# A four-layer attention and feed-forward kernel: the stack of a batch filled in four portions, its repeated rows stored once, four places for rows of maxima

## What is computed

```python
x = x + jnp.tanh(g_xattn[l]) * xattn_l(_layernorm(x, axis=-1), ctx_1024, ctx_1024)

# xattn, with 16 heads of 16 features, batch 8, 256 queries and 256 keys
scores = jnp.einsum('bhqd,bhkd->bhqk', q, k) / jnp.sqrt(16)
attn = jax.nn.softmax(scores, axis=-1)
x = jnp.einsum('bhqk,bhkd->bhqd', attn, v)
```

## Time and profile before

| | |
|---|---|
| Median of 3 runs | 1998.75 us (1997.51 to 2001.54) |
| The profiled execution's own time | 1983.74 us |
| Its span | 1981.9 us |
| Mean granted TensorE clock | 0.868 |
| TensorE matmul busy | 1470.5 us (74%) |
| VectorE busy | 1083.2 us (55%) |
| ScalarE busy | 735.4 us (37%) |
| GpSimd busy | 544.0 us (27%) |
| Moved by DMA | 202.65 MB, mean 102 GB/s |

### The profile page before, as it was taken

The page is one execution under the profiler, slowest core; times in us unless marked ns, Lnnn a source line. Parts: engine busy times, 40 slices in busy tenths (PEclk is TensorE's granted clock), DMA queues, the critical chain, the costliest instruction groups (busy, mean ns, idle before and its releaser), DMA issues.

```text
span 1981.9 us, 29494 instructions
## 1 busy us (share of the span) xinstructions
PE 1470.5 (74%) x9789; PEld 1035.4 (52%) x9816; DVE 1083.2 (55%) x2363; ACT 735.4 (37%) x1458; POOL 544.0 (27%) x519
## 2 busy tenths in 40 slices
PE   1489959986777349997996477942899755788676
PEld 1245548853445248887884244521788523455334
DVE  5256563346565515554537466581455556565797
ACT  2145644324555113332321255620344213554342
POOL 4342220021220353345315222007443431222000
PEclk9989979996789679998998688975999986779897
DMA  9989420099980241322126999012432593980000
GB/s 307 239 221 83 34 67 1 1 303 151 79 66 20 77 155 58 133 77 69 37 73 225 224 72 91 2 53 98 158 103 85 160 275 95 87 66 2 0 11 32
DMA packets 153868, 202.65 MB, mean 102 GB/s; under 512 B 19968, under 2 KB 113542, under 8 KB 153736
## 3 DMA queue, kind: packets, MB, share of 16 engines
q0 software_dynamic: 75392, 95.15, 33.7%
q1 hardware_dynamic: 78368, 106.05, 16.7%
HBM read 120.25 MB, written 80.35 MB: 101 GB/s over the span
## 4 chain that ended last, share of the span: by engine, by line
PE 48%; DMA 17%; DVE 15%; issue 8%; POOL 4%; ACT 4%; another core or an unknown queue 2%; SPq 2%; DVEq 0%; ACTq 0%; POOLq 0%
DMA stack<-mt 11%; PE PS L852 5%; PE PS L792 4%; PE PS L892 3%; PE PS L827 3%; PE PS L1030 2%; PE PS L1032 2%; PE PS L1031 2%; PE PS L1008 2%; PE PS L1009 2%; PE PS L1007 2%; PE PS L1018 2%; DVE xng L1583 2%; DVE amx L2139 1%
## 5 line engine op out<-in xcount | busy, mean ns | idle before, releaser
L1709 DVE TENSOR_REDUCE nm<-PS 128x2 f32<-128x512 f32 x512 | 336.8, 683 | 261.3 <-PE PS L792 165.5
L792 PE MATMUL PS<-stack 48*128 48x256 f32 x1024 | 154.9, 387 | 107.0 <-DVE nm L1709 56.4
L545 POOL DMA_DIRECT2D stack<-mt x128 | 70.0, 547 | 506.4 <-ACT mt L1294 505.8
L792 PEld LDWEIGHTS PS<-stack 48*128 48x128 f32 x1024 | 94.9, 228 | 204.8 <-DVE nm L1709 108.9
L1285 ACT ACTIVATE probs<-PS 128x512 f32<-128x512 f32 x256 | 139.0, 595 | 64.7 <-PE PS L835 31.8
L1285 ACT ACTIVATE xng<-PS 128x512 f32<-128x512 f32 x256 | 138.3, 591 | 46.6 <-PE PS L835 23.9
L852 PE MATMUL PS<-probs,vpad 128*32 128x256 f32 x1024 | 85.8, 462 | 71.3 <-ACT mt L1294 69.2
L827 PE MATMUL PS<-stack 49*128 49x256 f32 x1024 | 121.9, 319 | 19.7 <-DMA stack<-mt 15.2
L1031 PE MATMUL PS<-whi,hl 128*128 x468 | 133.2, 285 | 0.0
L1032 PE MATMUL PS<-wlo,hh 128*128 x468 | 133.2, 285 | 0.0
L1030 PE MATMUL PS<-whi,hh 128*128 x468 | 133.1, 284 | 0.0
(11 more groups left out here) (289 smaller groups left out, 3394.8 us busy)
## 6 DMA issues: line engine op xcount, KB each, us to landing
stack<-qk_parts POOLq DMA_DIRECT2D x128, 384.0 KB, 10.4
qk_parts<-k_parts SPq DMA_DIRECT2D x48, 512.0 KB
qk_parts<-q_parts SPq DMA_DIRECT2D x48, 512.0 KB, 10.9
wslot<-W_dram POOLq DMA_DIRECT2D x16, 1024.0 KB, 8.9
ys_sorted<-yo SPq DMA_DIRECT2D x78, 128.0 KB, 1.7
wide<-ctxT_dram SPq DMA_DIRECT2D x16, 512.0 KB, 5.8
wslot<-W_dram POOLq DMA_DIRECT2D x16, 512.0 KB, 6.1
xg<-xs_sorted SPq DMA_DIRECT2D x62, 128.0 KB, 2.1
```

The source lines that it names most:

```text
L792: mm = pe.matmul(PS[:, (2 * t + h) % 3, qt * S:(qt + 1) * S], q[rows, qt * P:(qt + 1) * P], kk[rows], start=(l > 0 or qt == 0), stop=(l > ...
L1709: nc.vector.tensor_reduce(nm[:, j % 2, at:at + 2], PS[:, (2 * t + h) % 3, :].rearrange("p (q n) -> p q n", q=2), AX.X, ALU.max, negate=Tru ...
```

## The change

Three things. The high parts are stored once: two stores for a group's keys and two for its queries in place of three each. The stack of a batch is filled in four portions (keys h 0, keys h 1, queries h 0, queries h 1) of two transfers each (16 rows, then 32 rows), one portion behind each row of maxima. And `mt` has four places with a semaphore each.

```diff
-        mt = sb("mt", [8, 2, P], F32R, at)
+        mt = sb("mt", [8, 4, P], F32R, at)
...
-                for r, part in enumerate((k_hi(g), k_hi(g), k_lo(g))):
+                for r, part in enumerate((k_hi(g), k_lo(g))):
...
-                for r, part in enumerate((q_hi(g), q_lo(g), q_hi(g))):
+                for r, part in enumerate((q_hi(g), q_lo(g))):
...
-            def load_stack(l, b):
-
-                if b >= SLOTS:
+            def load_stack(l, b, at):
+
+                of, h = (1, 0)[at // 2], at % 2
+                if at == 0 and b >= SLOTS:
                     pool.wait_ge(sc_mm, 2 * STEPS * l + 2 * PAIRS * (b - SLOTS + 1))
-                else:
+                if at == 0 and b < SLOTS:
                     nc.gpsimd.dma_start(stack[MAXROW:MAXROW + 65:64, b % SLOTS, 1].rearrange("p c n -> p (c n)"),
                                         io["ones_rows"]).then_inc(stack_in[b % SLOTS], 16)
-                for n, out in ((1, k_out), (0, q_out)):
-                    pool.wait_ge(*stored(out, l, b // 2))
-                    for h in range(2):
-                        nc.gpsimd.dma_start(stack[64 * h:64 * h + MAXROW, b % SLOTS, n],
-                                            parts[n, h][:, :, b * S:(b + 1) * S]).then_inc(stack_in[b % SLOTS], 16)
+                pool.wait_ge(*stored((q_out, k_out)[of], l, b // 2))
+                rows = lambda r, n: stack[64 * h + DH * r:64 * h + DH * (r + n), b % SLOTS, of]
+                part = parts[of, h][:, :, b * S:(b + 1) * S]
+                first, both = (0, 1) if of else (2, 0)
+                nc.gpsimd.dma_start(rows(first, 1), part[0:DH]).then_inc(stack_in[b % SLOTS], 16)
+                nc.gpsimd.dma_start(rows(both, 2), part).then_inc(stack_in[b % SLOTS], 16)
...
-                load_stack(l, 1)
-                load_stack(l, 2)
+                load_stack(l, 1, 0)
                 for n in range(QUADS):
...
                     put_rows(l, n)
-                    if n % 4 == 3 and n >= 7 and n // 4 + 2 < B:
-                        load_stack(l, n // 4 + 2)
+                    if (n + 5) // 4 < B:
+                        load_stack(l, (n + 5) // 4, (n + 1) % 4)
...
-                    pe.wait_ge(stack_in[b % SLOTS], 64 * loads + 16 * (l + 1))
+                    pe.wait_ge(stack_in[b % SLOTS], 128 * loads + 16 * (l + 1))
...
-                if j >= 2:
-                    act.wait_ge(row_in[j % 2], 16 * (j // 2))
-                nc.scalar.activation(mt[:, j % 2, :], PS[0:8, 6, S:S + P], ACT.Identity).then_inc(mt_done, 1)
+                if j >= 4:
+                    act.wait_ge(row_in[j % 4], 16 * (j // 4))
+                nc.scalar.activation(mt[:, j % 4, :], PS[0:8, 6, S:S + P], ACT.Identity).then_inc(mt_done, 1)
```

More of the change, by code:

```diff
@@ L259, in build @@
         ys = nc.dram_tensor("ys_sorted", (NT * P, D), F32, kind="Internal").ap()
-        parts = nc.dram_tensor("qk_parts", (2, 2, MAXROW, PAIRS, T), F32, kind="Internal").ap()
+        parts = nc.dram_tensor("qk_parts", (2, 2, 2 * DH, PAIRS, T), F32, kind="Internal").ap()
         PS = ctx.enter_context(nc.psum_tensor("PS", [P, 8, 512], F32))
@@ L279, in build @@
         stack_in = sem("stack_in", SLOTS)
-        mt_done, row_in = sem("mt_done"), sem("row_in", 2)
+        mt_done, row_in = sem("mt_done"), sem("row_in", 4)
         nat_mm, max_done = sem("nat_mm"), sem("max_done")
@@ L332, in stored @@
             n = GROUPS * l + g
-            return out[n % 2], 48 * (n // 2 + 1)
+            return out[n % 2], 32 * (n // 2 + 1)
         def rows_of(n, r, g):
@@ L545, in put_rows @@
                 nc.gpsimd.dma_start(stack[MAXROW:MAXROW + 65:64, b % SLOTS, 0, c:c + 2, :].rearrange("p c n -> p (c n)"),
-                                    mt[:, j % 2, :]).then_inc(row_in[j % 2], 16)
+                                    mt[:, j % 4, :]).then_inc(row_in[j % 4], 16)
             for l in lo_l:
@@ L576, in _ @@
                             make_mask(g)
-                    load_stack(0, 0)
+                    for at in range(4):
+                        load_stack(0, 0, at)
                     pool.wait_ge(v0_in, 16)
@@ L583, in _ @@
                 else:
-                    load_stack(l, 0)
-                load_stack(l, 1)
-                load_stack(l, 2)
+                    for at in range(4):
+                        load_stack(l, 0, at)
+                load_stack(l, 1, 0)
                 for n in range(QUADS):
@@ L819, in scores_key @@
                 j = s // 2
-                pe.wait_ge(row_in[j % 2], 16 * (j // 2 + 1))
+                pe.wait_ge(row_in[j % 4], 16 * (j // 4 + 1))
                 if s:
```

## The result

The change takes **2017.52 us** (median of 4 runs, 2014.10 to 2018.38), beside 1998.13 (1994.32 to 2001.54) of the kernel before: a ratio of 1.0108 [1.0083, 1.0134] (with its 95% interval), about +20 us. It is slower, inside the range and with the forecast sign, but less than half of the +45 us forecast.

The account below looks back on a forecast made before the run. It took the kernel as bound by waits for rows of maxima behind whole stacks, with low clock after them. Terms +43 (layers 1 to 3), +38 (layer 0), -35.5 (starts) gave +45 on the median 1998.75: 2044 us, range 2002 to 2085.

Parts of the forecast that it names:

- attention, layers 1 to 3: First to last row of maxima: seven waits of 7.95 us a layer, low clock included, 458.9 against 416.2: +43 us.
- attention, layer 0: Seven waits of 4.35 us, each with 1.9 of slow turns, plus 5 for portions meeting the store of zeros: +38 us.
- starts: Layer starts: fewer stores and fewer early portions give -17, -3, -4 and -11.5 us, together -35.5.
- The rows' 93.4 us: ScalarE's copy into `mt` waited 93.4 us in 20 places for earlier rows of maxima; forecast to go.
- portions didn't pile up: GpSimd's queue: 2.8 us per further transfer, under the 3.14 us turn, so no backlog; later and later landings would exceed the range.
- the two transfers of one didn't cost like two whole ones: Rival, chance 0.04: 16 and 32 rows each take 2.8 us, about +180 us, 2224; a portion's upper landing bound was 8.1.
- the clock didn't hold: Rival, chance 0.08: TensorE's granted clock stays at 1.00 behind the regular waits, 70 us fall away, giving 1974 us.
- Part 2: Each batch's last portion is late for TensorE: 5.3 landing plus 0.25 less 0.32 makes 5.25 us a wait.
- The low clock behind the wait: TensorE's turns after each wait in layers 1 to 3 run at the lower clock, costing 2.7 us a wait.
- Part 1: Attention: with one portion between rows and four places, the 135 us lost to rows of maxima go.
- 97.3 us: Attention of layers 1 to 3 without waits: thirty-one turns of 3.14 us from first to last row of maxima.
- estimate of 2.9 us for a portion: Rival that the portion lands early, chance 0.04: the skill's 2.9 us for 384 KB gives a sum of about 1977.

Follow-up runs that it names:

- e6: The change itself, unedited, run on the other chip: 1.0105 of the kernel before.
- e1: The kernel before, unedited, run again on another chip for the comparisons: 1938.1 us, 1.0003 of the kernel before.
- e5: The change, but with high parts stored three times and each portion one 48-row transfer: 1.0264 of the kernel before.
- e13: The change, with all four portions of batch 1 issued ahead of row 0 in place of one: 1.0033 of the kernel before.
- e10: The change, with 16 unread products on TensorE ahead of each wait for a stack but a layer's first: 0.9791 of the kernel before.
- e11: The kernel before with high parts stored once and transfers of 16 and 32 rows, whole stacks and two places: 0.9846 of the kernel before.
- e4: The kernel before with high parts stored once and four places, whole stacks kept (the change without portions): 0.9655 of the kernel before.
- e2: The kernel before with four places in `mt`, nothing else: 0.9809 of the kernel before.
- e9: The change with portions cut by pairs of heads, each half awaited apart, portions two rows earlier, three of batch 1 ahead of row 0: 1774.81 us, 0.9158 of before.
- e7: The change, with 30 unread products on TensorE ahead of each wait for a stack but a layer's first: 1.0118 of the kernel before.
- e8: The change with portions one row earlier, so the last is issued a turn sooner: 0.9577 of the kernel before.

## Why the prediction was right in sign and too high

The two columns of measurements are the pair of profiled executions on the first chip, and e6 less e1 on the other.

| term, us | forecast | first chip | other chip |
|---|---|---|---|
| attention, layers 1 to 3 | +43 | +25.5 | +20.8 |
| attention, layer 0 | +38 | +27.8 | +26.6 |
| starts | -35.5 | -19.6 | -32.3 |
| sum of the profiled spans | +45 | +33.7 | +14.8 |
| by the ratio of the runs | | +22 | +20 |

**The mechanism was right.** L795 waits at each of the 28 batches that aren't first, in all four layers, and for the last portion. The rows' 93.4 us are gone, and the rivals that put the queue or the clock differently fell: portions didn't pile up (L540 and L541 land in 3.7 and 4.1 us, the median of the page), the two transfers of one didn't cost like two whole ones (4.63 us in place of 8.1), and the clock didn't hold through waits of 4.4 us.

**The step that failed is the size of the wait in Part 2, 5.25 us.** Measured in layers 1 to 3 of the profile: 4.1 to 4.8, 4.39 on average. The landing is 4.63 us (median) in place of 5.3, and the first matmul follows it by 0.04 in place of 0.25; the lead of 0.31 was as I took it. The 5.3 came from a transfer of 48 rows in one, which lands in 5.05 (e5), while the change splits it in two. I had written "I take 5.3 because the bytes are the same", and the bytes did not decide. In 21 waits 0.86 us are 18, in layer 0 7 x 0.4 = 3 more. The low clock behind the wait was sized well: (441.6 - 291.9) / 21 = 7.13 us a wait in all, less 4.39 leaves 2.74, where I had 2.7. That is a remainder, which also holds the slow turns of a layer's start (e13); e10, in which most of the low clock is away, gives (444.3 - 393.5) / 21 = 2.4.

**Layer 0 by itself**: 38.9 us over its pace of 145.1, against 48.8. Of these 27.8 are waits (3.4 to 3.8, and one of 5.9 ahead of batch 3, whose portion took 7.02 us to land) and 11.1 the rest; I had 30.5 and 18.3. The slow turns and the store of zeros cost some 7 us less than my 1.9 a wait and 5 in one. That gives 18 + 3 + 7 = 28 us, the whole of the attention's miss on the first chip (81 - 53). On the other chip the miss is 34, and 7 of them are the kernel before: its layers 1 to 3 take 423.6 us there, where the prediction compared with 416.2.

**The starts** come to -32.3 on the other chip, where they can be read against e1, and by layer to -13.7, -3.8, -0.1, -14.2, where I had -17, -3, -4, -11.5; layer 2 gave nothing. In the pair on the first chip they are -19.6. These rest on one execution each, and I can't say which of the two is the truer; the runs in which only the stores change give -21.5 and -21.4 (e11, e4), those with the portions -15.9 (e5), and those with both -30.7 to -37.3 but for e13, which loads more ahead. On the other chip this term stood within its range of -50 to -20, on the first it ended just outside.

**The sum.** On the first chip 45 - 28 (attention) + 16 (starts) gives the +33 of the two profiled executions, and less the 14 us by which the one of before lay under its median +19, the difference of the medians. On the other chip 45 - 34 + 3 gives the +14.8 of the profiled pair; there the execution of e1 lay 5 us over the median of the kernel before, which leads to the +20 of the runs. On both, the attention's term carries the miss; on the first chip the 16 us by which the starts gave less and the 14 us of one execution nearly cancel, which is luck.

**What I would put otherwise** is Part 1. It said that 135 us were lost to the rows of maxima, and that they go. They go, but they weren't the rows' alone: e2 and e4 show a second wait just behind them, a stack that lands late. Only e9, where both are away, brings the layers near 97.3 us. That the prediction escaped this error is luck: the change put its own, larger wait in that place.

The Trainium skill (DMA: Bandwidth & Descriptors, Anatomy of one DMA) gives about 2.0 us and the bytes over 436 GB/s. Its estimate of 2.9 us for a portion would have made the change faster; measured were 5.05 in one transfer and 4.63 in two, so the trace disagrees, and the prediction was right to go by it. By the rule that I had cited for two transfers in place of one (the Trainium skill, SBUF — State Buffer, Door 1: The DMA port swizzle) the busiest ports are loaded as long either way; e5 and the change now show 5.05 and 4.63 us, so it holds only to within 0.4 us, and those 0.4 are half of what the wait was over-sized by.

## What to carry to other kernels

- Splitting a load into portions between small urgent transfers frees the small ones, but the last portion sets when the whole is there. Count from the end: the turn that needs it, less a landing, less the issue. Here one turn earlier was worth some 100 us of 1957.
- When a wait is taken away, ask what was late behind it. Whole stacks were four turns ahead, with 13.6 us to land in 12.6, and that showed only once the rows were out of the way.
- Where TensorE stopped for some 4.4 us again and again, more than half as much again (2.4 us, e10) was lost behind it in the clock. Products that ended just before the data landed gave that back (e10, 61 us); too many of them took it all (e7).

## What the runs showed of the hardware

- Two transfers of 16 and 32 partitions (128 and 256 KB) by one queue landed in 4.63 us from the first issue, one of 48 partitions (384 KB) in 5.05, though the second of the two was issued 0.52 us behind the first. Why is open.
- A wait of 4.5 us brought 6.9 us at the lower clock, part of it still in the wait. With the waits of 1.2 to 3.1 us of e8 the lower clock still covered 37 to 44 us of each of layers 1 to 3 (76 to 79 with the waits of 4.2 to 4.7 us of e6), with TensorE kept busy (e10) 13 to 21.
- The same kernel took 1998 us in the first pair and 1936 on each of the two chips of the experiments, with the attention alike within 6.3 us in the two profiles; between these the other stretches differed most from the attention of layer 1 to that of layer 2 (33 us) and from there to layer 3 (19 us).
